# Attention block before six windowed layers: early split, new order of the start, clears and splits moved between engines

## The reference

```
mod = (silu(c) @ wmod).reshape(4, 6, 1, -1)          # sa, ca, ga, sb, cb, gb
ga, gb = (2*(g >= 0) - 1) * max(|g|, 0.25)
h = layernorm(x) * (1 + ca) + sa
x = x + ga * attn(h)       # 16 heads of 8; low-rank q and kv; rope; softmax over all 512 keys; out @ Wo + bo
h = layernorm(x) * (1 + cb) + sb
x = x + gb * ffn(h)        # six layers, each: windowed attention (16 heads of 64, windows of 32, l2-normed q, k,
                           # rotary tables) on tokens shifted by one for half of the features, then a gated MLP
```

## Time and profile before

| | |
|---|---|
| median of 3 runs | 1975.84 us (1966.84 to 1978.34) |
| profiled execution | 1975.51 us, span 1973.7 us |
| PE busy | 1808.0 us (92%) |
| DVE busy | 1682.5 us (85%) |
| POOL busy | 1272.3 us (64%) |
| ACT busy | 1190.9 us (60%) |
| chain that ended last | DVE 37%, PE 34%, issue 10%, POOL 10%, ACT 8% |

### The profile page before, as it was taken

One profiled execution on the slowest core, in us unless ns is written; L12 is line 12 of the kernel. 1 busy time (PEld: TensorE's weight loads), 2 busy tenths in 40 slices (PEclk: granted clock), 3 DMA queues, 4 the chain that ended last, 5 costly groups with the idle time before them and its releaser, 6 DMA issues.

```text
span 1973.7 us, 49730 instructions
## 1 busy us (share of the span) xinstructions
PE 1808.0 (92%) x19284; PEld 1227.4 (62%) x19284; DVE 1682.5 (85%) x2794; ACT 1190.9 (60%) x2134; POOL 1272.3 (64%) x1650
## 2 busy tenths in 40 slices
PE   6999999789989999999999999999999999999986
PEld 2444444366666666666666676666666666676764
DVE  3777786799889989898999899998999899989982
ACT  1455566456666566656665666666656665666654
POOL 5112012577678777777876887767877778777761
PEclk9999999899999999999999999999999999999998
DMA  2000001345455555555555555545564546455552
GB/s 57 1 1 6 6 1 55 104 167 178 151 171 177 173 164 165 175 165 165 172 177 165 169 171 178 181 144 182 163 195 156 169 157 194 161 182 163 179 163 66
DMA packets 189287, 274.87 MB, mean 139 GB/s; under 512 B 23358, under 2 KB 85372, under 8 KB 188924
## 3 DMA queue, kind: packets, MB, share of 16 engines
q1 hardware_dynamic: 189052, 271.69, 42.4%
HBM read 71.33 MB, written 52.43 MB: 63 GB/s over the span
## 4 chain that ended last, share of the span: by engine, by line
DVE 37%; PE 34%; issue 10%; POOL 10%; ACT 8%; DMA 0%; SPq 0%; POOLq 0%; DVEq 0%; ACTq 0%
DVE turned L931 11%; DVE kz L951 11%; PE psum L558 4%; DVE rd L967 3%; PE psum L774 3%; PE psum L614 3%; PE psum L735 3%; POOL u L1313 3%; PE psum L637 3%; PE psum L560 2%; PE psum L559 2%; PE psum L746 2%; PE psum L714 2%; DVE smax L958 2%; PE psum L628 2%
## 5 line engine op out<-in xcount | busy, mean ns | idle before, releaser
L931 DVE SCALAR_TENSOR_TENSOR turned<-psum,vecs,tabs 128x1024 f32<-128x1024 f32 x384 | 487.9, 1271 | 18.4 <-POOL u L1313 6.8
L1108 ACT ACTIVATE sq<-psum 128x512 f32<-128x512 f32 x384 | 226.2, 589 | 112.3 <-PE psum L560 112.2
L1302 POOL TENSOR_TENSOR sdiff<-sdiff,rqs 128x512 f32<-128x512 f32 x192 | 201.1, 1047 | 126.9 <-DVE sdiff L963 121.2
L1313 POOL TENSOR_TENSOR qT<-turned,swapped 128x512 f32<-128x512 f32 x192 | 242.8, 1287 | 52.9 <-PE psum L714 50.7
L951 DVE TENSOR_TENSOR kz<-u,psum 64x512 f32<-64x512 f32 x384 | 259.4, 675 | 4.0 <-PE psum L702 0.7
L1313 POOL TENSOR_TENSOR u<-turned,swapped 128x512 f32<-128x512 f32 x192 | 242.1, 1282 | 14.6 <-DMA swapped<-turned 14.4
L1286 POOL TENSOR_TENSOR px<-px,rd 128x512 f32<-128x512 f32 x192 | 201.4, 1049 | 73.1 <-DVE rd L969 73.0
L558 PE MATMUL psum<-xs_hi,wqk_hi 128*128 128x512 f32 x384 | 183.6, 478 | 61.0 <-DVE turned L931 60.3
L735 PEld LDWEIGHTS psum<-pxT,v 128*64 128x64 f32 x6144 | 194.7, 138 | 69.5 <-issue 63.3
L735 PE MATMUL psum<-pxT,v 128*64 128x64 f32 x6144 | 221.2, 225 | 1.9 <-DMA pxT<-scratch 1.0
L746 PEld LDWEIGHTS psum<-onT,wo 128*128 128x128 f32 x1536 | 197.1, 191 | 21.4 <-issue 7.0
(11 more groups left out here) (182 smaller groups left out, 3710.2 us busy)
## 6 DMA issues: line engine op xcount, KB each, us to landing
swapped<-turned SPq DMA_DIRECT2D x384, 256.0 KB, 2.5
scratch<-pt SPq DMA_DIRECT2D x192, 256.0 KB, 2.2
pxT<-scratch SPq DMA_DIRECT2D x384, 128.0 KB, 2.9
v<-v SPq DMA_DIRECT2D x192, 192.0 KB, 2.5
w_raw<-in_wqkv SPq DMA_DIRECT2D x36, 256.0 KB, 3.1
v<-v SPq DMA_DIRECT2D x144, 64.0 KB, 2.2
wo<-in_wo SPq DMA_DIRECT2D x12, 256.0 KB, 3.3
w_raw<-in_w SPq DMA_DIRECT2D x12, 170.5 KB, 2.7
```

The lines of the kernel that those rows point to most:

```text
L931: engine.scalar_tensor_tensor(out=turned[:, n % NROT, :, :], in0=both, scalar=vec(("ks" if which else "qs", i)), in1=tabs[:, 2 * which:2 * ...
L1108: engine.activation(sq[:, n % NSQ, :], bank(n % 2), ACT.Square).then_inc(s_sq, 1)
L1302: engine.tensor_tensor(sdiff[:, :, :], sdiff[:, :, :], r_, ALU.mult).then_inc(s_weigh, 1)
L1313: engine.tensor_tensor(u[:, n % GT, :] if which else qT[:, m_, :], turned[:, n % NROT, 0, :], swapped[:, n % NSWAP, :], ALU.add).then_inc( ...
```

## The change

Numbers are split once per batch, before the packing. `qk` leaves its sum in `rot`; a new step `parts` lets ScalarE write the rounded part `qk_hi` and VectorE the remainder `qk_lo`. `pack` is then two fp32r products that add up in the bank: `selg[.., n, 0, ..]` has the rows that take the rounded part, `selg[.., n, 1, ..]` those that take the remainder. ScalarE alone reads the bank, into `q3` or `k_all`. `hi`, `lam`, `qkT` and `yT` go. `selg` is four times as large; it is loaded raw into `pT`, and GpSimd copies it to fp32r behind the first normalisation. VectorE clears `k3`, behind `mod`. The first normalisation stands ahead of `mod` on VectorE. SyncE loads batch 0 of x first and each later batch by itself; ScalarE issues ten of the weight transfers. Most early transfers have a semaphore of their own. In part B, GpSimd does both halves of `shift_parts`. Both tables of places have new numbers.

```diff
 PLACES_A = {
-    "xT": dict(tensor=-13.5, scalar=-13.5),
-    "norm": dict(vector=-11.9, scalar=-10.6, gpsimd=-12.7),
-    "hT": dict(tensor=-9.5, scalar=-9.2),
-    "ct": dict(tensor=-9.2, scalar=-9.1),
+    "mod": dict(tensor=-13.2, vector=-12.1, scalar=-15.2),
+    "xT": dict(tensor=-12.95, scalar=-12.75),
+    "norm": dict(vector=-12.7, scalar=-10.3, gpsimd=-11.85),
+    "hT": dict(tensor=-9.8, scalar=-9.8),
+    "ct": dict(tensor=-9.25, scalar=-9.15),
     "rope": dict(tensor=-8.9, vector=-8.7),
-    "qk": dict(vector=-8.2),
-    "v": dict(tensor=-6.6, vector=-6.3),
-    "pack": dict(tensor=-6.2, vector=-6.0, scalar=-6.0, gpsimd=-5.4),
+    "qk": dict(vector=-8.1),
+    "parts": dict(vector=-7.9, scalar=-7.9),
+    "v": dict(tensor=-4.9, vector=-4.55),
+    "pack": dict(tensor=-6.45, scalar=-6.45, gpsimd=-5.7),
...
-    "divide": dict(tensor=3.1, vector=3.3),
-    "oT": dict(tensor=9.7, scalar=9.5),
+    "divide": dict(tensor=3.45, vector=3.65),
+    "oT": dict(tensor=9.65, scalar=9.6),
...
-AFTER, UNIT = 33.3, 0.69
-EARLY = 11.1
+AFTER, UNIT = 33.9, 0.69
+EARLY = 10.8
 PLACES = {
-    "shift_parts": dict(vector=-0.05, gpsimd=-0.35),
+    "shift_parts": dict(gpsimd=-0.4),
-    "swap": dict(sync=0.45),
-    "rotate": dict(gpsimd=1.4),
+    "swap": dict(sync=0.75),
+    "rotate": dict(gpsimd=1.45),
-    "scale": dict(tensor=3.15, vector=3.25),
+    "scale": dict(tensor=3.1, vector=3.4),
-    "fetch": dict(sync=1.45),
-    "values": dict(tensor=1.1, scalar=1.45, gpsimd=1.3, sync=1.4),
+    "fetch": dict(sync=1.9),
+    "values": dict(tensor=1.05, scalar=1.4, gpsimd=1.75, sync=1.35),
-    "token_major": dict(tensor=4.35, scalar=5.0),
+    "token_major": dict(tensor=4.15, scalar=4.8),
-    "down": dict(tensor=9.1, vector=9.7),
+    "down": dict(tensor=9.3, vector=9.75),
...
# TensorE
-                engine.matmul(bk, selg[:, g, :], qkT[:, b % 2, n, :], start=True, stop=True).then_inc(fills, 1)
+                pe.wait_ge(s_selg, 1)
+                pe.wait_ge(s_qk_lo, nth_a["parts", b, n])
+                engine.matmul(bk, selg[:, n, 0, g, :], qk_hi[:, n, :], start=True, stop=False)
+                engine.matmul(bk, selg[:, n, 1, g, :], qk_lo[:, n, :], start=False, stop=True).then_inc(fills, 1)
...
# VectorE
+                for k_ in k3:                                          # end of "mod"
+                    engine.memset(k_[:, :, :, :].bitcast(F32), 0.0).then_inc(s_k3z, 1)
...
+            elif kind == "parts":
+                dve.wait_ge(s_qk_hi, nth_a[step])
+                engine.tensor_tensor(qk_lo[:, n, :], rot[:, 0, :], qk_hi[:, n, :].bitcast(F32), ALU.subtract)
-            elif kind == "pack":
-                dve.wait_ge(s_hi, nth_a[step])
-                engine.scalar_tensor_tensor(out=k_all[..] if n else q3[..], in0=hi[..], scalar=lam[..], in1=bk, ...)
-            elif kind == "shift_parts":
-                engine.tensor_tensor(lo_, rT[rows, f % B, 0:T - late], hi_.bitcast(F32), ALU.subtract)
...
# ScalarE
+        engine.dma_start(wq3[:, :, :], ...)      # then wuk, wk2, ropec, ropes, wuv, bv, onesc, wo_a, selg_raw
...
+            elif kind == "parts":
+                act.wait_ge(s_qk, nth_a[step])
+                if b:
+                    act.wait_ge(*bank_a.full("pack", b - 1, n, NG - 1))
+                engine.copy(qk_hi[:, n, :], rot[:, 0, :]).then_inc(s_qk_hi, 1)
             elif kind == "pack":
-                engine.activation(hi[:, :], bk, ACT.Identity, bias=onesc[:, 0:1] if n else 0.0).then_inc(s_hi, 1)
+                if n:
+                    engine.activation(k_all[:, g % 2, :], bk, ACT.Identity, bias=onesc[:, 0:1]).then_inc(empties, 1)
+                else:
+                    engine.copy(q3[b % 2][:, g, :], bk).then_inc(empties, 1)
...
# GpSimd
-                    for k_ in k3:
-                        engine.memset(k_[:, :, :, :].bitcast(F32), 0.0).then_inc(s_fill, 1)
+                    pool.wait_ge(s_a, 16 * 10)
+                    engine.tensor_copy(selg[...], selg_raw).then_inc(s_selg, 1)
...
-                rows, late = halves[0]
+                for j, (rows, late) in enumerate(halves):
+                    pool.wait_ge(s_xhi, 2 * f + j + 1)
+                    engine.tensor_tensor(lo_, rT[rows, f % B, 0:T - late], hi_.bitcast(F32), ALU.subtract)
+                    pool.wait_ge(s_xlo, 2 * f + j + 1)
...
# SyncE
+        engine.dma_start(x0[:, 0:TT, :], ...).then_inc(s_x[0], 16)   # then wmod, cT, ident, vecs, wdq, wdkv, x0 of 1 to 3
```

More of the change, by code:

```diff
@@ L146, in put @@
             timed.append((place + PLACES_A[step[0]][engine], len(timed), step))
+    put(0, "mod")
     for b in range(B):
@@ L168, in order_a @@
                     put(place + half + c / 2, "weighted", b, g, half, c)
-    start = [(-20.0, ("mod",))] * (engine in ("tensor", "vector", "scalar"))
-    return start + [(place, step) for place, _, step in sorted(timed)]
+    return [(place, step) for place, _, step in sorted(timed)]
 def tile(n):
@@ L431, in build @@
     for step in plan_a["scalar"]:
-        if step[0] in ("xT", "hT", "ct", "oT", "norm2", "rT"):
+        if step[0] in ("xT", "hT", "ct", "pack", "oT", "norm2", "rT"):
             bank_a.drain("act", *step)
     for step in plan_a["vector"]:
-        if step[0] in ("mod", "rope", "v", "pack", "maxima", "peaks", "divide", "proj"):
+        if step[0] in ("mod", "rope", "v", "maxima", "peaks", "divide", "proj"):
             bank_a.drain("dve", *step)
     norms_a = [step for step in plan_a["vector"] if step[0] in ("norm", "norm2")]
-    s_const = sem("s_const_loaded")
-    s_x = sem("s_x_loaded")
+    s_const, s_ident, s_wmod = sem("s_const_loaded"), sem("s_ident_loaded"), sem("s_wmod_loaded")
+    s_k3z = sem("s_k3_zeros")
+    s_x = [sem(f"s_x{b}_loaded") for b in range(B)]
+    s_c, s_down = sem("s_c_loaded"), sem("s_wd_loaded")
     s_a = sem("s_weights_a_loaded")
@@ L916, in vector @@
                     engine.memset(pxT[:, :, :, :, :, :], 0.0).then_inc(s_pxT_clear, 1)
-            elif kind == "shift_parts":
-                f, = k
-                rows, late = halves[1]
-                hi_, lo_ = (w_[rows, f % NXS, WIN + late:] for w_ in (xs_hi, xs_lo))
-                dve.wait_ge(s_xhi, 2 * f + 2)
-                engine.tensor_tensor(lo_, rT[rows, f % B, 0:T - late], hi_.bitcast(F32), ALU.subtract).then_inc(s_xlo[1], 1)
             elif kind == "heads":
```

173 lines of the change are left out of this document (85 added, 88 removed).

## The result

The changed kernel takes 1947.23 us (median of 4 runs, 1944.70 to 1951.52), the kernel before in the same comparison 1971.38: ratio 0.988, 95% interval 0.985 to 0.991. The forecast was 1944, in a range from 1908 to 1968. The profiled execution took 1951.5 us around a span of 1949.7, against 1975.5 and 1973.7, so 24.0 us are to be accounted for.

The account below looks back on a forecast made before the run. Bounds: latencies in the start, TensorE in the attention, TensorE and VectorE close together in the layers. Terms summed to -29.9, with -2 for bank waits -31.9, on 1975.5: 1944 us, full range 1908 to 1968, chance 0.54.

Parts of the forecast that it names:

- Start: Up to the first maxima: earlier first normalisation and shorter packs, less added splits and held key ropes, -5.3 us.
- the size of the clears: Start: clearing k3 on VectorE takes 7.0 us per tensor, 14.1 for both, ending at 26.3.
- Packs and corrections: Attention: 32 packs as two fp32r matmuls save TensorE 11.7 us beyond the start; VectorE's dropped corrections save 5.3.
- splits: Attention: eight added splits of 1.3 us each, on the chain twice behind 60 us, +2.6.
- banks: Attention: maxima no longer wait for a bank held by a correction, -2 us.
- Between the stages: From attention to layers: the first heads matmul comes behind the last oT, +2 us.
- Layers' relief: Layers: VectorE's half of the split goes to GpSimd; 14 blocks gain 0.87 us each, -12.2.
- Order in the layers: Layers: new places only exchange neighbours on engines, charged at nothing, bounds 10 us either way.
- More is won: Rival: VectorE's relief counts whole in the layers, TensorE's idle time in attention shrinks, better order; 1921 us, chance 0.15.
- Only the attention gains: Rival: another wait fills the 0.87 us gap, so the layers stay where they are; 1956 us, chance 0.15.
- GpSimd becomes the bound: Rival: GpSimd is on the chain at the layers' splits, losing 12.2 us and adding 19; 1975 us, chance 0.09.
- Swaps come late: Rival, layers: swaps issue behind v's two copies; half of 192 lose 0.65 us, +62, 2006 us, chance 0.07.

Follow-up runs that it names:

- e5: The kernel before, with only VectorE's half of xs_lo moved to GpSimd, which does both halves in a row: 1956.90 us, ratio 0.994.
- the last experiment: The changed kernel with the swap's old place, old base numbers, both clears on GpSimd, first xn and its transposes ahead of x's: 1935.83 us, ratio 0.983.

## Why the prediction was right, and where its steps were not

- **Start, -5.3: came as -3.7.** The chain up to TensorE's first rotary product gained more than forecast: 25.90 before, 19.93 after, so 6.0 instead of 4.8, since the transfer issues ran beside the table load. The step that failed is the size of the clears: the row of 0.86 ns per element left out the 0.38 us ahead of it and stood for 1.04, and the ropes came 2.1 us after the forecast 26.
- **Packs and corrections, -11.7 and -5.3, splits +2.6, banks -2: -16.4, came as -17.5.** The total is nearer than its parts can be checked. TensorE's term stood for the whole 11.7, and by the doubled products 8.8 to 11.8 of it count. VectorE's terms come to 4.7 (5.3 and 2, less 2.6), and by the added operations 5.4 to 7.9 of its 18.2 us count. So the pieces of the chain undervalued somewhat an engine that is busy 40 of 50 us; that two errors cancel is likely and not shown.
- **Between the stages, +2: came as +4.9.** Here one late step was priced, the first heads product, and the swap behind it was not. Some 2 us of the excess go with the swap's place; the base number is not shown to cost anything, and the rest is open.
- **Layers' relief, -12.2: measured alone -11.1.** The argument, that TensorE's 0.87 us would be late next in the blocks where VectorE's half was on the chain, gave the size. (The chain has 14 such pieces, not 15, and two of them, at 450.77 and 514.07, lie before the mark of block 0: 12 x 0.87 is 10.4.) The picture behind it was only partly right: "they slow each other" holds for GpSimd's half, but what VectorE's 1.48 us met was GpSimd's multiplication of `px`. With the half gone from VectorE, both meetings are gone.
- **Order in the layers, 0 within 10 either way: came as 0 to +3, out of +6 to +10 and -6 to -8.** This is the step that failed in kind: that no exchange of neighbours costs anything. Each of the two was nearly as large as the bound for all, and one of them was on the table: the rival of late swaps named the place, the queue and the sign in the waits, but was priced as all (62 us) or nothing. Its signs came (the swap went out 6.9 us late in one step, and the waits for swapped rows rose from 14.4 to 42.2 us), and its cost was 6 to 10 us. That the two nearly cancelled is luck.
- **The rivals.** "More is won" needed the old place of the swap and one clear on GpSimd: 1930 is what was measured with them and the old base numbers, still above its 1921. "Only the attention gains" is refuted by e5, and "GpSimd becomes the bound" by the same: its two halves cost no time that shows. "Swaps come late" holds at a sixth of its price or less.

So the forecast stands 3 us from the median, and 8 us from the profiled execution, since the executions of before that it was made against were 4 us above the median of this comparison (1975.5 against 1971.38). That the forecast is only 3 us off is in part luck of this kind: it promised 31.9 us, and 24 came, or 20 to 22 against the other medians of before. The four stretches were off by 1.6, 1.1, 2.9 and 4.5 us; the two large terms, packs and relief, carried it. The bounds that the prediction names add up to 1969 at the top, not to 1965.

## What to carry to other kernels

A table of new places is a change by itself: split it by queue before believing its sum, and look in the trace for a transfer that is issued microseconds after its data is ready. Where two engines slow each other, look which instruction of the other engine was running at that moment. When an engine loses work, price it in two ways, by its pieces on the chain and by its busy share, and measure it with idle work put back at the same place. A row's duration is not its hold on the engine: take the distance between the starts of two neighbours.

## What the runs showed of the hardware

- A VectorE clear of 128x8192 float32 reads 6.88 us in its row and holds the engine for 8.54 (the distance of two starts); the missing 1.66 stands ahead of it as "issue". For 128x2048 it is 1.76 and 0.38. On GpSimd the row of 128x8192 reads 6.93, and in the last experiment the VectorE operation that stood still beside it ended with it (14.38 and 14.36).
- A clear on GpSimd stopped VectorE's small `tensor_scalar` from and to SBUF for 3.99 us (0.17 in the changed kernel), and let its copy out of PSUM (0.18) pass.
- In the start, the same three 64x512 float32 products, six passes, took 5.45 us in one execution and 2.81 in another, both with a granted clock of 1.00 from 20 to 25 us: 0.91 and 0.47 us a pass, a factor of two, as between TensorE's two levels of 1.2 and 2.4 GHz, which the granted clock doesn't show here. Behind the quick one the granted clock fell to 0.50 from 30 to 35 us. It moves the first maxima by 4 us between two kernels with one and the same start (40.63 and 36.58).
- VectorE's half of `xs_lo` (64x511) took 0.71 us with nothing beside it and 1.48 when it started 0.1 us behind GpSimd's multiplication of `px`, which kept its 1.05. GpSimd's half (64x512) took 1.72 when it started while VectorE's ran, up to 1.29 when it came first, and a median of 1.18 in the kernels where VectorE's is gone.
